# Perceiver block on one core: batch 0's last two head pairs ahead of batch 1's, and its distance stage inside the last step

## The chip, the cores and the metric

The kernel runs on one core of a Trainium2 chip. The metric is the device time of one execution in microseconds (us); less is better. The engines are TensorE (PE; its weight loads are listed as PEld), VectorE (DVE), ScalarE (ACT), GpSimd (POOL) and SyncE (SP), which issues all DMAs.

## The reference

Two batches of 256 tokens with 256 channels pass through three residual blocks. Cut to what matters:

```python
def reference(x, ctx, wq, wk, wv, wo, aq, ak, av, ao, Wg, bg, W1, b1, W2, b2):
    # 1 cross attention, 16 heads of 64, over 4096 context rows per batch
    q, k, v = heads(layernorm(x) @ wq), heads(ctx @ wk), heads(ctx @ wv)
    x = x + merge(softmax(q @ k.T / 8) @ v) @ wo
    # 2 self attention over 256 tokens, 16 heads of 16, by hyperbolic distance
    h = layernorm(x)
    q, k, v = heads(h @ aq.T), heads(h @ ak.T), heads(h @ av.T)
    denom = maximum((1 - |q|^2) * (1 - |k|^2), 1e-6)
    cosh_arg = maximum(1 + 2 * (|q|^2 + |k|^2 - 2 q @ k.T) / denom, 1)
    x = x + merge(softmax(-arccosh(cosh_arg)) @ v) @ ao.T
    # 3 eight experts; each token takes the one with the greatest gate
    h = layernorm(x)
    idx = argmax(softmax(h @ Wg + bg))
    y = gelu(h @ W1 + b1) @ W2 + b2        # per expert
    return x + take(y, idx)
```

## The kernel before

Every instruction is placed by hand: each engine has its own program, and semaphores link them.

**Cross attention** takes 16 steps, n = 0 to 15, one for a pair of heads `hp` and a batch `b`, in the order (0,0), (0,1), (1,0) up to (7,1). A step has 32 slots, one for 128 context rows. In a slot TensorE multiplies the scores (L1357, L1359), ScalarE takes their exponentials to fp32 (L1525) and in three slots of four to fp16 (L1523; in the fourth VectorE casts them, `split_p`, L1685), GpSimd subtracts the fp16 part from the fp32 one (L1826), and three slots later (LAG) TensorE multiplies probabilities and values, 12 short matmuls (`pv`, L1374 to L1379). Beside this TensorE projects the keys, the row maxima and the first values of the next step (`CHUNKS`, `MAX_AT`); scores have two PSUM banks and fp32 probabilities four buffers, so that no engine runs far ahead. The output of step n - 1 is normalised, turned, projected and added in slots 3 to 12 of step n.

The last step (n = 15, batch 1) prepares no further step. In its slots stand the layernorm of batch 0 (`LN_AT`), its transposes (`XT_AT`), the transposes of the four self attention weights (`TURN_AT`) and the split of the expert weights to fp16 high and low parts (`EXPERTS_AT`: high on ScalarE L768, low on VectorE L773, 8 each).

**Self attention** (`tail_pe`, `tail_act`, `tail_dve`, `tail_pool`) comes after the last `pv`. Per batch: *rows* i = 0 to 7, the projected queries and keys of four heads with their lengths (PE `qk` L570 and `lengths` L580, L584; ACT `squares` L788 and `rows` L797; DVE `low_rows` L965); *inverses*, twelve short VectorE instructions (L988 to L1004) for 1/(1 - length) in three bf16 parts; *placing* them (PE L605, ACT L808, DVE L1011), with a matrix `place` that GpSimd builds; 16 *distance units* m (PE L639, L641; DVE `ratios` L1028, L1031, two instructions of 128x512); then for each of four groups two roots (ACT L833, L835), their sum (POOL L457), logarithm and exponential (ACT L840, L848), and the `average` of the values with its transposes (L652, L662). `RATIO` names four buffers for eight groups. The rows of batch 1 are interleaved with the first units of batch 0. After that come output projection, a layernorm, the gate and the experts.

## Time and profile before

| | us |
|---|---|
| time, median of 3 runs | 1189.27 (1186.86 to 1191.82) |
| the profiled execution's own time | 1191.87 |
| its span, first to last instruction | 1190.1 |
| TensorE busy | 1082.1 (91% of the span) |
| ScalarE busy | 898.2 (75%) |
| VectorE busy | 814.0 (68%) |
| GpSimd busy | 696.8 (59%) |

Busy time is the union of an engine's instructions. The clock granted to TensorE is given as a share of full speed, 1.00 for 2.4 GHz and 0.50 for 1.2 GHz; its mean over the span is 0.947. Times of rows are counted from the start of the span.

### The profile page before, as it was taken

Reading aid. Unit: us, or ns where it says so; the run is one execution under the profiler, and the core shown is the slowest. Engines: PE = TensorE matmul, PEld = TensorE weight load, DVE = VectorE, ACT = ScalarE, POOL = GpSimd, SP = SyncE. Lnnn points to the kernel's source line nnn. Section 1 sums busy time; section 2 is a strip of 40 time slices with the busy share of each in tenths; the row PEclk is TensorE's granted clock in tenths of the full one; section 3 lists DMA queues with packets and bytes.
Section 4 is the critical chain, followed back from the end, with each engine's and each line's share of the span. In section 5 each row is a group of like instructions: output and inputs, shape, how many; then the busy total and the mean of one; then the engine's idle time right before and its main releaser. Section 6 shows DMA issues by size and latency. Waiting matters only on the chain.

```text
span 1190.1 us, 33353 instructions
## 1 busy us (share of the span) xinstructions
PE 1082.1 (91%) x13853; PEld 787.1 (66%) x13853; DVE 814.0 (68%) x1180; ACT 898.2 (75%) x1608; POOL 696.8 (59%) x603
## 2 busy tenths in 40 slices
PE   5789999999999999999999999999999878736698
PEld 3467777767677777676777777777777757412455
DVE  5878777686868686868686868777776445856322
ACT  5787888888888878788878787878887864478533
POOL 5567666666666666666666666666666780335023
...
DMA packets 32487, 42.00 MB, mean 35 GB/s; under 512 B 2874, under 2 KB 26962, under 8 KB 32338
## 3 DMA queue, kind: packets, MB, share of 16 engines
...
## 4 chain that ended last, share of the span: by engine, by line
PE 73%; DVE 10%; ACT 8%; issue 5%; POOL 3%; DMA 0%; DVEq 0%; ACTq 0%; POOLq 0%
PE ps L1261 12%; PE ps L1291 12%; PE ps L1357 8%; PE ps L1359 8%; PE ps L1374 6%; PE ps L1312 6%; PE ps L1379 5%; PE ps L1377 4%; DVE m_part L1659 3%; PE ps L704 2%; POOL psums L1826 2%; ACT probs L1525 2%; PE ps L722 2%; PE ps L1340 1%; PE ps L570 1%
## 5 line engine op out<-in xcount | busy, mean ns | idle before, releaser
L1826 POOL TENSOR_TENSOR psums<-probs 128x512 f16<-128x512 f32 x512 | 594.7, 1173 | 312.2 <-ACT probs L1525 171.2
L1525 ACT ACTIVATE probs<-ps 128x512 f32<-128x512 f32 x512 | 304.8, 599 | 52.7 <-PE ps L1359 52.0
L1659 DVE TENSOR_REDUCE m_part<-ps 128x2 f32<-128x1024 f32 x256 | 311.9, 1221 | 29.0 <-PE ps L1312 26.0
L1357 PE MATMUL ps<-q,k 128*128 128x256 f16 x1024 | 252.1, 273 | 5.6 <-ACT probs L1525 5.5
L1374 PE MATMUL ps<-v_sb,probs 128*128 128x65 f16 x2048 | 242.2, 194 | 15.4 <-issue 9.1
L1359 PE MATMUL ps<-q,k 128*128 128x256 f16 x1024 | 252.0, 273 | 0.0
L1523 ACT ACTIVATE probs<-ps 128x512 f16<-128x512 f32 x384 | 229.1, 597 | 22.2 <-PE ps L1359 18.3
L1377 PE MATMUL ps<-v_sb,probs 128*128 128x64 f16 x2048 | 240.1, 192 | 0.0
L1379 PE MATMUL ps<-v_sb,psums 128*128 128x65 f16 x2048 | 239.2, 194 | 0.0
L1374 PEld LDWEIGHTS ps<-v_sb,probs 128*128 128x128 f16 x2048 | 189.1, 98 | 68.8 <-issue 41.0
L1649 DVE TENSOR_TENSOR k<-ps,k 64x512 f16<-64x512 f32 x256 | 176.4, 689 | 51.8 <-ACT k L1480 47.6
L1480 ACT ACTIVATE k<-ps 64x512 f16<-64x512 f32 x256 | 151.4, 592 | 62.8 <-PE ps L1261 57.7
L1377 PEld LDWEIGHTS ps<-v_sb,probs 128*128 128x128 f16 x2048 | 191.0, 97 | 5.0
L1379 PEld LDWEIGHTS ps<-v_sb,psums 128*128 128x128 f16 x2048 | 191.1, 97 | 0.0
L1291 PE MATMUL ps<-wv_hi,ctx_lo 128*128 128x128 f16 x1024 | 184.9, 219 | 0.0
L1291 PE MATMUL ps<-wv_lo,ctx_hi 128*128 128x128 f16 x1024 | 184.7, 219 | 0.0
L1291 PE MATMUL ps<-wv_hi,ctx_hi 128*128 128x128 f16 x1024 | 184.5, 219 | 0.1
L1678 DVE TENSOR_TENSOR v_sb<-ps,v_sb 128x512 f16<-128x512 f32 x128 | 88.2, 690 | 107.2 <-ACT v_sb L1486 107.2
L1357 PEld LDWEIGHTS ps<-q,k 128*128 128x128 f16 x1024 | 100.2, 98 | 40.9 <-ACT probs L1525 6.5
L1359 PEld LDWEIGHTS ps<-q,k 128*128 128x128 f16 x1024 | 100.4, 98 | 34.3
L1312 PE MATMUL ps<-k,q 64*128 64x512 f16 x512 | 99.5, 386 | 12.0 <-DVE m_part L1659 12.0
L1291 PEld LDWEIGHTS ps<-wv_hi,ctx_hi 128*128 128x128 f16 x1024 | 100.4, 98 | 0.6 <-DVE v_sb L1678 0.3
...
## 6 DMA issues: line engine op xcount, KB each, us to landing
...
```

The costliest lines, as they stand in the source:

```text
L1291: mm = pe.matmul(ps[:, bank, t * P:(t + 1) * P], y[:, par, c, toks], w[:, par, c, :], start=(k == 0), stop=(k == 5))
L1312: mm = pe.matmul(ps[:, bank + 1 - h, :], q1[rows, par, h, t * P:(t + 1) * P], k1[rows, par, h, 512 * j:512 * (j + 1)], start=True, stop=True)
L1357: pe.matmul(ps[:, SC + s % 2, cols], k1[:, par, h, keys], q1[:, par, h, :], start=True, stop=False)
L1359: mm = pe.matmul(ps[:, SC + s % 2, cols], k2[:, par, h, keys], q2[:, par, h, :], start=False, stop=True)
L1374: pe.matmul(out, p_hi[:, s % NP, h, queries], value[:, XD:2 * XD + 1], start=(s == 0 and h == 0 and t == 0), stop=False, skip_group_check= ...
L1377: pe.matmul(ps[:, ACC, at:at + XD], p_hi[:, s % NP, h, queries], value[:, 0:XD], start=False, stop=False, skip_group_check=True)
L1379: mm = pe.matmul(out, p_lo[:, s % NP, h, queries], value[:, XD:2 * XD + 1], start=False, stop=(s == SLOTS - 1), skip_group_check=True)
L1523: nc.scalar.activation(p_hi[:, s % NP, :, :], scored, ACT.Exp, scale=XSCALE)
L1525: nc.scalar.activation(p_raw[:, s % NX, :, :], scored, ACT.Exp, scale=XSCALE) \
L1649: i = nc.vector.tensor_tensor(k1[other, par, h, keys], ps[rows, bank, :], k1[rows, par, h, keys], ALU.subtract)
L1659: nc.vector.tensor_reduce(m_part[:, j, t, :], ps[:, bank:bank + 2, :], AX.X, ALU.max) \
L1826: nc.gpsimd.tensor_tensor(p_lo[:, s % NP, :, :].rearrange("p h q -> p (h q)"), p_raw[:, s % NX, :, :].rearrange("p h q -> p (h q)"), p_hi[ ...
```

## The change

The order of the steps is the same up to step 11; then come (6,0), (7,0), (6,1), (7,1), so that batch 0 is complete one step earlier (`ORDER`, `DONE0` = 14). A step's buffers go by its parity now, not by its batch. GpSimd builds `place` (half as wide, 12 copies of 64 partitions) within step 13. Step 14, which is a full step with a successor, takes in addition batch 0's layernorm, the transposes of its rows and of the four weights, with the same PSUM bank (PM) for all. The weights' DMAs and the first expert matrix are issued ahead of step 15's key copies, the second one when four low parts are done. Step 15 takes batch 0's rows in slots 0 to 8, inverses (11 instructions now) in slots 9 to 11, placing in 14 and 15, and distance units 0 to 15 in slots 16 to 31. Four expert quarters are split in slots 1 to 7; the other high parts in slots 26 to 29, two low parts in 26 and 28, and the last two low parts after the step among batch 1's rows. What remains behind the last `pv` is batch 1's rows, inverses, placing and 16 units, and all roots, logarithms, exponentials and averages. Batch 0's roots stand among batch 1's rows on ScalarE; its averages stand among batch 1's units. `ratio` has eight buffers, and sums, logarithms and exponentials are made in place.

```diff
+ORDER = tuple((i // 2, i % 2) for i in range(STEPS - 4)) + tuple(
+    (hp, b) for b in range(B) for hp in (HP - 2, HP - 1))
+DONE0 = STEPS - 2
...
-TURN_AT = {20: 0, 23: 1, 27: 2, 29: 3}
-TURN_BANK = (MX, MX + 1, PK, MX)
-TURN_X = (PK, PM)
-RATIO = (0, 1, 3, 0, 1, 0, 2, 1)
-EXPERTS_AT = (13, 15, 18, 21, 27, 28, 30, 31)
+TURN_AT = {14: 0, 17: 1, 23: 2, 26: 3}
+XT_AT, VARIANCE_AT, ROOT_AT, NORMALISED_AT = 20, 13, 14, 15
+ZERO_AT = 5
+PLACE_AT = {4: None, 8: 0, 11: 1, 14: 2, 17: 3, 20: 4, 23: 5}
+INVERSES_AT = {9: (0, 1, 2, 3), 10: (4, 5, 6, 7), 11: (8, 9, 10)}
+PLACED_AT = {14: (0, 1), 15: (2, 3)}
+UNITS = 16
+UNIT_AT = {16 + m: m for m in range(UNITS)}
+HIGH_AT = {1: 0, 3: 1, 5: 2, 7: 3, 26: 4, 27: 5, 28: 6, 29: 7}
+LOW_AT = {1: 0, 3: 1, 5: 2, 7: 3, 26: 4, 28: 5}
+LATE_LOW_AT = {2: 6, 5: 7}
 OUT_BANKS = ((6, 7), (0, 1))
 XN_BANK, GATE_BANK = 2, 3
-AVERAGE_AT = (24, 27)
-PLACE_BANKS = ((0, 1), (4, 5))
-ROWS_AHEAD = 3
-LN_AT, ROOT_AT, XT_AT = 13, 15, 18
+ROOT_PART_AT = (1, 3, 5, 7)
+AVERAGE_AT = (24, 26, 28, 30)
+ROW_BANKS = ((4, 7), (4, 5, 7))
+PLACE_BANKS = (((4, 7), (3, 6)), ((4, 5), (4, 5)))
+PAIRS = ((3, 6), (0, 2))
 SPLIT_K_AT, SPLIT_V_AT = 16, 12
...
-        ratio = [m.rearrange("p (k h q) -> p k h q", k=2, h=4)
-                 for m in (k1_32[:, 6144:8192], lo32[:, 0:2048], v32[:, 0:2048],
-                           k2_32[:, 6144:8192])]
...
+        halves = [m[:, 4096:8192].rearrange("p (k s w) -> p s k w", k=2, s=2) for m in (k1_32, k2_32)]
+        ratio = [halves[0][:, 0, :, :], halves[1][:, 0, :, :],
+                 lo32[:, 4096:6144].rearrange("p (k w) -> p k w", k=2),
+                 lo32[:, 6144:8192].rearrange("p (k w) -> p k w", k=2),
+                 v32[:, 0:2048].rearrange("p (k w) -> p k w", k=2),
+                 halves[0][:, 1, :, :], halves[1][:, 1, :, :],
+                 hi32[:, 0:2048].rearrange("p (k w) -> p k w", k=2)]
...
-            sp.wait_ge(s_v, (STEPS - 1) * KCH)
-            for i, w in enumerate((aq, ak, av, ao)):
-                sp.dma_start(a_raw[:, i, :, :], w.rearrange("(t p) n -> p t n", p=P)).then_inc(s_aw, 16)
-            sp.wait_ge(s_sc, (STEPS - 1) * SLOTS)
-            for raw, w in ((w2_raw, w2), (w1_raw, w1)):
-                sp.dma_start(raw.rearrange("p (m n) -> p m n", n=F),
-                             w.rearrange("e (c p) n -> p (e c) n", p=P)).then_inc(s_ew, 16)
...
             if w == 0:
                 pe.wait_ge(s_aw, 4 * 16)
-                pe.wait_ge(s_red, STEPS * NU)
-                pe.wait_ge(s_ya, STEPS - 1)
+                pe.wait_ge(s_ya, DONE0)
+            else:
+                pe.wait_ge(s_ac, w)
             if w == 2:
...
+        def qk(pe, i, b):
+            w, g = divmod(i, 4)
+            if (b, i) == (0, 0):
+                pe.wait_ge(s_ac, 2)
+                pe.wait_ge(s_xc, NC + 1)
+                pe.wait_ge(s_vl, (STEPS - 1) * KCH + 2)
+                pe.wait_ge(s_red, STEPS * NU)
+            if (b, i) == (1, 0):
+                pe.wait_ge(s_xc, NC + 2)
+                pe.wait_ge(s_rt, 2 * 16)
+                pe.wait_ge(s_vl, STEPS * KCH)
+            if i >= len(ROW_BANKS[b]):
+                pe.wait_ge(s_lx, 8 * b + i - len(ROW_BANKS[b]) + 1)
+            for c in range(NC):
+                mm = pe.matmul(ps[:, row_bank(i, b), 0:TQ],
+                               aqk_T[:, w, c, 4 * g:4 * g + 4, :].rearrange("p h d -> p (h d)"),
+                               xnT[:, c, b * TQ:(b + 1) * TQ],
+                               start=(c == 0), stop=(c == NC - 1))
+            mm.then_inc(s_qk, 1)
+
...
+        def place_rows(pe, b, g):
+            if g == 0:
+                pe.wait_ge(s_iq, IQ * (b + 1))
+                pe.wait_ge(s_lx, 8 * (b + 1))
+            if (b, g) == (0, 0):
+                pe.wait_ge(s_tc, PLACED)
+                pe.wait_ge(s_ya, STEPS - 1)
+            for w in range(2):
+                if b == 0 and g >= 2:
+                    pe.wait_ge((s_pq, s_pk)[w], g - 1)
+                if b == 1 and g >= 1:
+                    pe.wait_ge((s_pq, s_pk)[w], 4 * b + g)
+                rows = slice(64 * w, 64 * w + 64)
+                for i in range(3):
+                    mm = pe.matmul(ps[:, PLACE_BANKS[b][g % 2][w], 0:TQ], place[rows, i, g, :],
+                                   inv_p[rows, i, :], start=(i == 0), stop=(i == 2))
+                mm.then_inc(s_pl, 1)
...
-            pe.wait_ge(s_tc, TC)
-            rows_step(0, 0)
             last_output()
-            for i in range(1, 9):
-                rows_step(i, 0)
-            pe.wait_ge(s_or, STEPS)
+            pe.wait_ge(s_ya, STEPS)
             transposes_batch(pe, 1)
-            values(1)
-            for i in range(ROWS_AHEAD):
-                rows_step(i, 1)
-            pe.wait_ge(s_tc, TC + 2)
-            place_rows(0)
...
+            for i in range(9):
+                multiply_rows(pe, i, 1)
+                if i == 0:
+                    pe.wait_ge(s_or, STEPS)
+                    values(1)
+            for g in range(4):
+                place_rows(pe, 1, g)
...
-            for m, gg, b, g, kt, jj in attn_units():
-                if m == 16:
-                    place_rows(1)
-                distances(m, b, g, kt, jj)
-                if ROWS_AHEAD + m < 9:
-                    rows_step(ROWS_AHEAD + m, 1)
+            for m, gg, b, g, kt, jj in attn_units()[16:]:
+                distances(pe, m, b, g, kt, jj)
                 if m in AVERAGE_AT:
-                    average(AVERAGE_AT.index(m), 0, AVERAGE_AT.index(m))
-            turn_average(0, 0, 0)
-            for g in range(2, 4):
-                average(g, 0, g)
-                turn_average(g - 1, 0, g - 1)
+                    i = AVERAGE_AT.index(m)
+                    average(i, 0, i)
+                    if i >= 1:
+                        turn_average(i - 1, 0, i - 1)
...
-            for b in range(B):
-                for g in range(4):
-                    if (b, g) == (0, 0):
-                        for i in range(ROWS_AHEAD, 9):
-                            rows_step(i, 1)
-                    roots(4 * b + g)
-                for g in range(4):
-                    logarithms(4 * b + g, g)
-                    if b == 0:
-                        take_placed(1, g)
-                    if (b, g) == (1, 2):
-                        take_turned_xn(1, 0, OUT_BANKS[0][0])
-                for g in range(4):
-                    weights(4 * b + g, g)
+            act.wait_ge(s_vone, 2)
+            take_turned_output()
+            take_values(0)
+            root_of_product(0)
+            root_of_variance(act, 2, slice(2, NT))
+            root_of_sum(0)
+            take_batch(act, 1)
+            take_rows(act, 0, 1)
+            take_values(1)
+            for i in range(1, 9):
+                take_rows(act, i, 1)
+                if i in ROOT_PART_AT:
+                    gg, part = divmod(2 + ROOT_PART_AT.index(i), 2)
+                    (root_of_product, root_of_sum)[part](gg)
+            roots(3)
+            for gg in range(3):
+                logarithms(gg)
+            for g in range(4):
+                take_placed(act, 1, g)
+            logarithms(3)
+            for gg in range(4):
+                weights(gg)
+            for gg in range(4, 8):
+                roots(gg)
+            for gg in range(4, 8):
+                logarithms(gg)
+                if gg == 6:
+                    take_turned_xn(1, 0, OUT_BANKS[0][0])
+            for gg in range(4, 8):
+                weights(gg)
...
+            def step(n):
+                par, (hp, b) = n % 2, ORDER[n]
+                if n + 2 < STEPS:
                     sp.wait_ge(s_q, n + 1)
                     sp.wait_ge(s_wkl, n + 1)
-                    load_wqk(b, hp + 1)
-                if prepares(hp, b):
+                    load_wqk(par, ORDER[n + 2][0])
+                if more_after(n):
                     at_least(sp, s_wvl, n)
-                    load_wv(1 - b, hp + b)
+                    load_wv(1 - par, ORDER[n + 1][0])
                 at_least(sp, s_yx, n - 1)
-                load_wo(b, hp)
-                if prepares(hp, b):
-                    copy_k2(n + 1, 1 - b)
-
-            for hp in range(HP):
-                step(hp, 0)
-                step(hp, 1)
+                load_wo(par, hp)
+                if n == DONE0:
+                    sp.wait_ge(s_v, DONE0 * KCH)
...
                         turn_weights(pe, TURN_AT[s])
+                    if not more:
+                        if s <= 8:
+                            multiply_rows(pe, s, 0)
+                        for i in PLACED_AT.get(s, ()):
+                            place_rows(pe, 0, i)
+                        if s in UNIT_AT:
+                            m, gg, _, i, kt, jj = units[UNIT_AT[s]]
...
-                    if s in EXPERTS_AT and not more:
-                        split_experts_high(act, EXPERTS_AT.index(s))
+                    if not more:
+                        if s <= 8:
+                            take_rows(act, s, 0)
+                        if s in HIGH_AT:
+                            split_experts_high(act, HIGH_AT[s])
+                        for i in PLACED_AT.get(s, ()):
+                            take_placed(act, 0, i)
...
+                    if n == DONE0 and s == VARIANCE_AT:
+                        dve.wait_ge(s_ya, DONE0)
+                        variance(1, slice(0, 2))
+                    if n == DONE0 and s == NORMALISED_AT:
+                        normalised(1, slice(0, 2))
+                    if not more:
+                        if 1 <= s <= 8:
+                            low_rows(dve, s - 1, 0)
+                        for k in INVERSES_AT.get(s, ()):
+                            inverses(dve, 0, k)
+                        if s in LOW_AT:
+                            split_experts_low(dve, LOW_AT[s])
+                        for i in PLACED_AT.get(s, ()):
+                            take_placed_keys(dve, 0, i)
+                        if s in UNIT_AT:
+                            m, gg, _, i, kt, jj = units[UNIT_AT[s]]
+                            ratios(dve, m, gg, 0, kt, jj)
...
```

`multiply_rows`, `take_rows`, `low_rows`, `inverses`, `take_placed` and `distances` are the functions of before, moved out of the tail and called from both places.

On VectorE, the first slots of step 15 before the change (n = 15, probabilities, output and values alone):

```order
L1685 CAST probs<-probs 128x512 [waits s_pv,s_exp]
L1693 COPY o_acc<-ps 128x264 [waits s_on,s_pv]
L1698 RECIPROCAL o_rcp<-o_acc 128x4 [waits s_or]
L1701 TENSOR_TENSOR o_norm<-o_acc,o_rcp 128x2x2x64 [waits s_tt,s_rs]
L1685 CAST probs<-probs 128x512 [waits s_pv,s_exp]
L1678 TENSOR_TENSOR v_sb<-ps,v_sb 128x8x64 [waits s_vc]
L1685 CAST probs<-probs 128x512 [waits s_pv,s_exp]
L1678 TENSOR_TENSOR v_sb<-ps,v_sb 128x8x64 [waits s_vc]
L1711 TENSOR_TENSOR x_sb<-x_sb,ps 128x512 [waits s_ya,s_yx]
```

and with it:

```order
L1703 CAST probs<-probs 128x512 [waits s_pv,s_exp]
L953 SCALAR_TENSOR_TENSOR k<-ps,vecs,k 128x256 [waits s_qx]
L773 SCALAR_TENSOR_TENSOR k<-ctx_hi,k 128x1024 [waits s_eh]
L953 SCALAR_TENSOR_TENSOR k<-ps,vecs,k 128x256 [waits s_qx]
L1711 COPY o_acc<-ps 128x264 [waits s_on,s_pv]
L953 SCALAR_TENSOR_TENSOR k<-ps,vecs,k 128x256 [waits s_qx]
L773 SCALAR_TENSOR_TENSOR k<-ctx_hi,k 128x1024 [waits s_eh]
L1716 RECIPROCAL o_rcp<-o_acc 128x4 [waits s_or]
L1719 TENSOR_TENSOR o_norm<-o_acc,o_rcp 128x2x2x64 [waits s_tt,s_rs]
L953 SCALAR_TENSOR_TENSOR k<-ps,vecs,k 128x256 [waits s_qx]
L1703 CAST probs<-probs 128x512 [waits s_pv,s_exp]
L1696 TENSOR_TENSOR v_sb<-ps,v_sb 128x8x64 [waits s_vc]
```

The low rows (L953) and the low parts of the experts (L773) now stand between the casts, the output of step 14 and the values. Later in the same step, from slot 18 on before the change:

```order
L1685 CAST probs<-probs 128x512 [waits s_pv,s_exp]
L773 SCALAR_TENSOR_TENSOR ctx_hi<-k,ctx_hi 128x1024 [waits s_eh]
L1678 TENSOR_TENSOR v_sb<-ps,v_sb 128x8x64 [waits s_vc]
L1685 CAST probs<-probs 128x512 [waits s_pv,s_exp]
L773 SCALAR_TENSOR_TENSOR ctx_hi<-k,ctx_hi 128x1024 [waits s_eh]
L1685 CAST probs<-probs 128x512 [waits s_pv,s_exp]
L1678 TENSOR_TENSOR v_sb<-ps,v_sb 128x8x64 [waits s_vc]
L773 SCALAR_TENSOR_TENSOR ctx_hi<-k,ctx_hi 128x1024 [waits s_eh] x2
L1685 CAST probs<-probs 128x512 [waits s_pv,s_exp]
L773 SCALAR_TENSOR_TENSOR ctx_hi<-k,ctx_hi 128x1024 [waits s_eh] x2
L1693 COPY o_acc<-ps 128x264 [waits s_on,s_pv]
```

and the end of placing with units 0 to 4 (slots 15 to 20) with it:

```order
L986 CAST wqk_raw<-ps 128x256 [waits s_pl] x2
L1003 TENSOR_SCALAR k<-ps 128x512 [waits s_sc,s_dd]
L1005 SCALAR_TENSOR_TENSOR k<-ps,k 128x512 [waits s_rt]
L1703 CAST probs<-probs 128x512 [waits s_pv,s_exp]
L1003 TENSOR_SCALAR k<-ps 128x512 [waits s_dd]
L1005 SCALAR_TENSOR_TENSOR k<-ps,k 128x512 [waits s_rt]
L1003 TENSOR_SCALAR k<-ps 128x512 [waits s_dd]
L1005 SCALAR_TENSOR_TENSOR k<-ps,k 128x512 [waits s_rt]
L1696 TENSOR_TENSOR v_sb<-ps,v_sb 128x8x64 [waits s_vc]
L1003 TENSOR_SCALAR k<-ps 128x512 [waits s_dd]
L1005 SCALAR_TENSOR_TENSOR k<-ps,k 128x512 [waits s_rt]
L1003 TENSOR_SCALAR k<-ps 128x512 [waits s_sc,s_dd]
```

Each slot from 16 on now has two instructions of a unit that wait for TensorE (s_dd), and later casts and values are queued behind them. On ScalarE, from the last exponentials on, before the change:

```order
L1525 ACTIVATE probs<-ps 128x512 [waits s_lo]
L768 ACTIVATE ctx_hi<-k 128x1024
L780 ACTIVATE psums<-ps 128x16x16 [waits s_vp,s_vone]
L780 ACTIVATE psums<-ps 128x16x16
L1493 ACTIVATE o_turn<-ps 128x256 [waits s_yx,s_tt]
L788 ACTIVATE ctx_lo<-ps 128x256 [waits s_qk] x2
L797 ACTIVATE k<-ps,vecs 128x256 [waits s_nm]
L788 ACTIVATE ctx_lo<-ps 128x256 [waits s_sl,s_qk]
L797 ACTIVATE k<-ps,vecs 128x256 [waits s_nm]
```

and with it:

```order
L1507 ACTIVATE o_turn<-ps 128x256 [waits s_yx,s_tt,s_vone]
L809 ACTIVATE psums<-ps 128x16x16 [waits s_vp]
L809 ACTIVATE psums<-ps 128x16x16
L820 ACT_TABLE_LOAD [waits s_pv]
L820 ACTIVATE probs<-k 128x2048 [waits s_rt]
L751 ACTIVATE rstd<-var 128x2 [waits s_ln]
L823 ACTIVATE k<-k,vecs 128x2x1024
L507 ACTIVATE xnT<-ps 128x2x256 [waits s_xt]
L780 ACTIVATE ctx_lo<-ps 128x256 [waits s_sl,s_qk]
L809 ACTIVATE psums<-ps 128x16x16 [waits s_vp]
L809 ACTIVATE psums<-ps 128x16x16
L780 ACTIVATE ctx_lo<-ps 128x256 [waits s_sl,s_qk]
```

The output of step 15 is taken first, then the first root of batch 0 (L820) with its table load stands ahead of the layernorm's root (L751), and the rows of batch 1 follow.

## Rows read from the trace of the kernel before

**Rows 1.** Stretches: length, busy us of PE, PEld, DVE, ACT, POOL, clock, DMA.

```profile
863.70:920.70 57.00, 56.06 (x800) 41.80 (x799) 41.85 (x57) 46.20 (x89) 36.88 (x33) 1.00 0.18 45
920.70:974.50 53.80, 41.47 (x678) 36.27 (x676) 26.91 (x38) 43.89 (x78) 42.91 (x37) 0.91 0.24 77
1029.80:1091.00 61.20, 29.39 (x254) 12.59 (x258) 46.12 (x67) 43.20 (x28) 27.38 (x6) 0.50 0.00 0
1091.00:1190.10 99.10, 79.51 (x471) 47.59 (x463) 27.04 (x72) 49.26 (x59) 27.46 (x18) 0.81 0.02 6
```

**Rows 2.** Groups in step 15: busy, mean ns, idle before.

```profile
L773 DVE SCALAR_TENSOR_TENSOR ctx_hi<-k,ctx_hi 128x1024 f16<-128x1024 f32 x8 | 12.1, 1512 | 8.5 <-ACT ctx_hi L768 8.5
...
L752 ACT ACT_TABLE_LOAD x1 | 1.3, 1283 | 0.0
```

**Rows 3.** TensorE in step 15 in order of time: start, duration, idle before.

```profile
930.23 0.20 PE L1374 MATMUL ps<-v_sb,probs 128*128 128x65 f16 x1 [1.10 <-POOL psums L1826]
...
930.60 0.27 PE L1357 MATMUL ps<-q,k 128*128 128x256 f16 x1
...
930.93 0.27 PE L1359 MATMUL ps<-q,k 128*128 128x256 f16 x1
...
946.17 0.39 PE L1357 MATMUL ps<-q,k 128*128 128x256 f16 x1 [4.03 <-ACT probs L1525]
```

**Rows 4.** TensorE in the rows of batch 0, then of batch 1.

```profile
987.77 1.03 PE L570 MATMUL ps<-xnT,ctx_lo 128*128 128x256 f32 x4
...
989.50 1.03 PE L570 MATMUL ps<-xnT,ctx_lo 128*128 128x256 f32 x4
...
998.33 0.60 PE L505 MATMUL ps<-ident,xn 128*128 128x128 f32 x4
...
1011.08 2.07 PE L570 MATMUL ps<-xnT,ctx_lo 128*128 128x256 f32 x4
...
1014.79 0.83 PE L639 MATMUL ps<-k 32*128 32x256 f16 x6
```

**Rows 5.** VectorE: inverses of batch 0, placing, one inverse of batch 1.

```profile
999.01 0.41 DVE L988 TENSOR_SCALAR ctx_lo<-ps 128x256 f32<-128x256 f32 x1
...
1004.45 0.42 DVE L1004 TENSOR_TENSOR ctx_lo<-ctx_lo 128x256 f32<-128x256 f32 x1
...
1008.48 0.42 DVE L1011 CAST k<-ps 128x256 bf16<-128x256 f32 x1 [0.59 <-PE ps L605]
...
1032.43 3.29 DVE L992 TENSOR_TENSOR ctx_lo<-ctx_lo 128x256 f32<-128x256 f32 x1
```

**Rows 6.** VectorE in batch 1's units, and an average among them.

```profile
1072.14 0.68 DVE L1028 TENSOR_SCALAR k<-ps 128x512 f32<-128x512 f32 x1
...
1073.46 0.68 DVE L1028 TENSOR_SCALAR k<-ps 128x512 f32<-128x512 f32 x1
...
1079.22 0.42 DVE L1038 COPY ctx_lo<-ps 128x256 f32<-128x256 f32 x1 [0.39 <-PE ps L652]
1080.19 0.69 DVE L1028 TENSOR_SCALAR v_sb<-ps 128x512 f32<-128x512 f32 x1 [0.54 <-PE ps L641]
```

**Rows 7.** ScalarE and GpSimd in the units of batch 0 and the exponentials.

```profile
1030.81 4.64 POOL L457 TENSOR_TENSOR k<-probs,k 128x2048 f32<-128x2048 f32 x1 [50.16 <-ACT k L835]
...
1042.03 1.91 ACT L833 ACTIVATE probs<-k 128x2048 f32<-128x2048 f32 x1 [7.33 <-DVE k L1031]
...
1067.00 7.31 ACT L848 ACTIVATE k<-k 128x2048 f32<-128x2048 f32 x4
```

**Rows 8.** From the last pv to batch 1's layernorm.

```profile
980.67 0.66 ACT L780 ACTIVATE psums<-ps 128x256 f32<-128x256 f32 x2 [9.79 <-POOL psums L449]
...
983.48 0.69 DVE L1711 TENSOR_TENSOR x_sb<-x_sb,ps 128x512 f32<-128x512 f32 x1 [7.83 <-PE ps L1340]
...
990.17 0.74 DVE L1591 BATCH_NORM_STATS2 stats<-x_sb 128x6 f32<-128x256 f32 x2
...
992.73 0.74 DVE L1610 TENSOR_SCALAR xn<-x_sb,mv,rstd 128x256 f32<-128x256 f32 x2
```

608 lines of the change are left out of this document (285 added, 323 removed).

## The prediction

> **What bounds the kernel now.** I read the stretches first, then TensorE's timeline in the last step, then all engines in order of time behind the last pv. In step 14 TensorE is busy 56.1 of 57.0 us at clock 1.00 [rows 1]: a full step is bound by TensorE, and whatever it is given there is added to the time. Step 15 (920.7 to 974.5) is not: TensorE is busy 41.5 of 53.8 us, and none of the four others is full [rows 1]. One wait of 4.03 us stands in it, where the layernorm and its two table loads of 1.28 us hold up the exponentials [rows 2, 3]. Behind the last pv (974.5) the engines take turns. From 1029.8 to 1091.0 TensorE is busy 29.4 of 61.2 us at clock 0.50, VectorE 46.1, ScalarE 43.2, GpSimd 27.4 [rows 1]: VectorE works on units while ScalarE waits 7.33 us for four of them [rows 7], then ScalarE works while VectorE waits. So the end is set by a serial chain of VectorE and ScalarE that lasts 116.5 us from the last pv to the last unit, and 99.1 us more to the end of the span [rows 1]. Those 99.1 us (roots of the last group, logarithms, exponentials, output, gate, experts) hold the same operations before and after the change; I leave them as they are. So I need three terms: step 14, step 15, and the stretch from the last pv to the last unit.
>
> **Steps 0 to 13: nothing.** The order of batches changes which context columns are read, not how many. In step 13 GpSimd gets a memset and 12 small copies; it is busy only 36.9 of 57 us in a full step [rows 1], so they lie beside TensorE. If that cover were gone they would cost at most the 4.9 us between the last pv and GpSimd's memsets (974.5 to about 979.4; ScalarE's 9.79 us wait in [rows 8] contains them).
>
> **Step 14: +3 us.** TensorE gets 20 transposes. Four of them took 0.60 us with their drain [rows 4], some 0.44 in a row: 5 x 0.44 = 2.2 us, all on the path, as TensorE is the bound. ScalarE gets two table loads (2.6), five evictions of 0.5 to 0.6 (2.8) and the root: 46.2 + 5.7 = 52 of 59 us, so it has room on average, but in slot 14 it waits for the transposes and then reloads its table. TensorE has two slots of 1.8 us before it needs that exponential, which covers most of it; I take 0.8 us. Bounds: 2.2 (all covered) and 6 (the 4.03 us wait of [rows 3] comes back in part). The transposes of the rows stand five slots behind the layernorm now and wait for nothing. SP issues four weight loads and a 2 MB load ahead of step 15's key copies; the copies' data exist only from the middle of step 14, so they are not delayed.
>
> **Step 15: +17 us.** Slots 0 to 8. TensorE's work in a slot: pv 0.35 (930.23 to 930.60 with its issue) and scores 0.44 (four at 0.11) [rows 3], and one cycle of rows, 1.73 (987.77 to 989.50) [rows 4]: 2.5 us, and 0.64 more in two slots with values. Now the links. `qk` of cycle i + 1 needs the bank that low row i - 1 frees (two banks, three in the tail), and that row goes from TensorE's length over ScalarE (0.47) to VectorE (0.48). ScalarE also has exponentials (0.95) and in four slots an expert quarter (about 1.0); in slot 3 VectorE takes the old output behind a low part, and pv waits for it about 1 us. By laying these out slot by slot I get 24 us for the nine slots. Slots 9 to 15: the inverses are a VectorE chain, 999.01 to 1005.2 before [rows 5], 5.9 us with one instruction less, plus a cast and values; they must be done at slot 14, for placing. Two groups of placing in a slot take about 1 us (one lasted 1.01 [rows 5]); 15 us for seven slots. Slots 16 to 31: a unit costs VectorE 1.32 us (1072.14 to 1073.46) [rows 6]. 16 x 1.33 = 21, four casts 1.8, two values 1.4, two low parts at 1.5 each 3.0 [rows 2], and 1.5 us because unit 8 writes where context values are still read until slot 25: 29 us. TensorE's share of such a slot (0.8 and 0.5 for a unit) fits. Three more pv: 3. Sum 24 + 15 + 29 + 3 = 71, against 53.8: +17. Bounds: TensorE's own sum, about 56 us with all that it is given, plus waits of 8 (+10), and +26 if each slot of the rows takes 3.2 us and each unit's slot 2.0. The stall of 4.03 us is gone from this step and is already in the difference.
>
> **From the last pv to the last unit: 116.5 becomes 77 us, -39.5.** (a) Batch 1's xnT is ready 12 us behind the last pv: before, the output was added at 984.2 (9.7 us) after a wait for GpSimd's place work [rows 8]; without that work I take 7.5, then 3.3 for the layernorm (990.17 to 993.47) [rows 8], 0.6 for transposes, 0.6 for the eviction. (b) Rows of batch 1 alone: nine cycles of 1.73 are 15.6, values 2; ScalarE's four root parts of 1.9 [rows 7] fit into two cycles each with little over, and TensorE has just idled, so some of it runs at clock 0.50; I add 2.4: 20 us. (c) Then ScalarE has two roots, a table load and three logarithms before it takes a placed row: 3.9 + 1.3 + 5.7 = 11 us; VectorE's inverses (5.9, and two waits of 2.9, see below) run beside that and are level with it. (d) Placing 4 x 1.05 and the first unit: 5 us. (e) 16 units, 21.2 us; four averages among them: one cost VectorE 1.4 us (from 1078.8, the end of a unit, to the start of the next at 1080.19) [rows 6], with a transpose behind it at clock 0.50 2.0: 1.4 + 3 x 2.0 = 7.4. Sum 12 + 20 + 11 + 5 + 28.6 = 76.6. What is saved is batch 0's rows, inverses, placing and 16 units, whose roots now run where ScalarE idled. Bounds: 69 (root parts hidden, averages 1.4 each) and 91 (the two rivals on this stretch together).
>
> One rule speaks against (c). The inverse at 1032.43 took 3.29 us instead of the 0.42 of its like [rows 5], and it lies within a GpSimd addition of 4.64 us that began at 1030.81 [rows 7]: 2.9 us of waiting. My sum has two such waits. The Trainium skill, page "SBUF — State Buffer", section "🔬 SBUF: two separate sides", states an exclusive lock: a VectorE operation with two SBUF inputs and a GpSimd operation that reads SBUF block one another for the whole instruction. By that rule, the trace agrees, all five such instructions that now stand in this stretch (two late low parts, three inverses) can wait, not two; that is the port rival below.
>
> **The sum.** +3 + 17 - 39.5 = -19.5. On the profiled execution (span 1190.1, own time 1191.87) that is a span of 1170.6 and a time of 1172.4; its own time lies 2.6 us over the median of 1189.27, so against the median I say 1170.
>
> **Rivals.** *Slower: TensorE falls to 1.2 GHz in step 15.* Its place is slots 0 to 8, where it now waits for ScalarE and VectorE in each slot. At clock 0.50 a cycle of rows took 3.71 us (1011.08 to 1014.79) [rows 4] against 1.73: 8 x 2.0 = 16, and scores and pv double, 9 x 0.8 = 7: +23, 1193 us. It decides from 19 us on, that is if some four fifths of these slots run so. For it: in the old units, clock 0.50 stayed for 61 us. Against it: in step 15 TensorE is busy 77% of the time and the mean clock is still 0.91 [rows 1]; it fell once, with the 4.03 us idle stretch [rows 3], and the new step keeps it busier. Chance 0.10, of which half is partial and ends within 0.5%.
>
> *The rows in the tail run at 1.2 GHz.* They begin after some 4 us of idle TensorE, and ScalarE's root parts keep interrupting. 8 x (3.71 - 1.95) = 14: 1184 us. Against it: they are almost back to back on TensorE. Chance 0.10.
>
> *The port rival.* Three more waits of 2.9 us: +9, 1179 us. Against it: GpSimd is free for much of (b). Chance 0.08.
>
> *More than I say.* Links in step 15 overlap better than my slot by slot layout (+12), and (b) to (e) take 70: 1158 us. Chance 0.13.
>
> *The forecast itself,* 1163 to 1178: 0.59.
>
> **Numbers.** 0.5% is 5.9 us, about what a measurement of this kernel can tell from no change: below 1183.3 is faster, above 1195.2 slower. Of the slower rival 0.05 counts as slower, 0.05 as same; of the 1.2 GHz rows 0.04 as same. Faster 0.86, same 0.09, slower 0.05. The range 1160 to 1184 leaves out half of the better case (0.07) and the slower rival (0.10).
>
> **What the profile will show.** Step 14 lasts 60 us instead of 57, with ScalarE's wait in slot 14. Step 15 lasts about 71, at clock near 1.00, with 2.7 us a slot at first and 1.8 in the units. From the last pv to the last unit 77 us, ScalarE without a 7 us wait among batch 0's roots, and 99 us after it. I am wrong if TensorE shows clock 0.50 in step 15, if casts queued behind units starve GpSimd and pv, or if the 99 us stretch, which I did not cost, moves.

## The result and the profile after

The changed kernel takes 1170.82 us (median of four runs, 1167.91 to 1171.87) against 1189.43 (1186.86 to 1191.82, four runs) on the same chip: a ratio of 0.984, 95% interval 0.9812 to 0.9868. That is 18.6 us less; 19.4 were forecast, from 1189.27 to 1170. The profiled execution took 1171.87 us, its span is 1170.2, and 1170.6 was forecast for the span.

The windows of the changed kernel, with the columns of [rows 1]: step 14, step 15, then three pieces of step 15, then pieces of the tail, and last the stretch behind the last unit.

```profile
864.00:928.10 64.10, 60.01 (x818) 45.12 (x817) 46.09 (x69) 51.00 (x97) 38.12 (x37) 0.97 0.12 33
928.10:1000.20 72.10, 65.55 (x875) 54.10 (x874) 50.00 (x79) 48.21 (x90) 38.34 (x33) 0.93 0.10 31
...
928.10:952.90 24.80, 24.20 (x256) 21.05 (x255) 12.80 (x20) 19.99 (x40) 11.08 (x10) 1.00 0.01 2
952.90:967.60 14.70, 11.77 (x170) 9.88 (x167) 10.72 (x20) 8.40 (x18) 7.98 (x7) 0.88 0.46 145
967.60:1000.20 32.60, 29.59 (x453) 23.17 (x454) 26.48 (x41) 19.82 (x34) 19.29 (x16) 0.90 0.01 2
1000.20:1013.90 13.70, 7.83 (x28) 5.83 (x28) 4.45 (x16) 7.10 (x9) 5.71 (x9) 0.75 0.01 2
1013.90:1030.90 17.00, 13.74 (x64) 11.62 (x62) 7.29 (x13) 15.54 (x23) 6.61 (x2) 0.99 0.00 0
1030.90:1046.30 15.40, 4.17 (x32) 1.97 (x36) 10.96 (x13) 10.91 (x11) 6.96 (x2) 0.50 0.00 0
1046.30:1070.80 24.50, 18.80 (x200) 8.47 (x192) 22.24 (x37) 22.29 (x13) 9.58 (x3) 0.70 0.01 2
1070.80:1170.20 99.40, 75.11 (x437) 46.52 (x437) 26.09 (x70) 49.25 (x59) 26.91 (x18) 0.81 0.02 6
```

Against [rows 1]: step 14 is 7.1 us longer, step 15 18.3 us longer, the 116.5 us from the last pv to the last unit are 70.6, and what follows them lasts 99.4 instead of 99.1. TensorE is busy 65.6 of 72.1 us in step 15, where it was busy 41.5 of 53.8: the work went to where four engines had had room. All terms: +0.2 ahead of step 14, +7.1, +18.3, -45.9, +0.3, together -20.0, which is the difference of the spans (1190.1 and 1170.2) to rounding.

In step 14 three waits of TensorE stand that were not there before. TensorE in step 14 of the changed kernel:

```profile
894.13 0.39 PE L1313 MATMUL ps<-k,q 64*128 64x512 f16 x2 [0.77 <-DVE m_part L1677]
...
895.92 0.28 PE L1362 MATMUL ps<-q,k 128*128 128x256 f16 x1 [0.28 <-ACT probs L1539]
...
900.84 0.61 PE L1313 MATMUL ps<-k,q 64*128 64x512 f16 x2 [2.42 <-DVE m_part L1677]
```

The largest waits for VectorE's maxima (L1677), since they free the PSUM pair of the scores. So ScalarE and VectorE are read next, each in order of time:

```profile
891.49 1.28 ACT L751 ACT_TABLE_LOAD   x1
892.78 0.20 ACT L751 ACTIVATE rstd<-var 128x2 f32<-128x2 f32 x1
...
893.49 1.28 ACT L1537 ACT_TABLE_LOAD   x1
...
895.75 0.60 ACT L1500 ACTIVATE v_sb<-ps 128x512 f16<-128x512 f32 x1
```

```profile
892.76 1.23 DVE L1677 TENSOR_REDUCE m_part<-ps 128x2 f32<-128x1024 f32 x1
896.39 0.69 DVE L1696 TENSOR_TENSOR v_sb<-ps,v_sb 128x512 f16<-128x512 f32 x1 [2.40 <-ACT v_sb L1500]
897.00 0.15 DVE L1622 RECIPROCAL rstd<-rstd 128x2 f32<-128x2 f32 x1
...
897.58 1.02 DVE L1625 TENSOR_SCALAR newton<-newton 128x2 f32<-128x2 f32 x1
...
898.83 0.73 DVE L1628 TENSOR_SCALAR xn<-x_sb,mv,rstd 128x256 f32<-128x256 f32 x2
899.48 1.22 DVE L1677 TENSOR_REDUCE m_part<-ps 128x2 f32<-128x1024 f32 x1
```

This is one chain over three engines. The two table loads, 2.6 us, make ScalarE late with the values; VectorE stands idle for them (2.40 us), then does the root's Newton step and the normalisation (897.00 to 899.5) and only then takes the maxima on which TensorE waits 2.42 us. Behind that wait the granted clock is 0.50 from 900.8 to 904.2. One instruction of the Newton step, L1625, takes 1.02 us for two numbers per partition, where its neighbours take 0.16. It starts within a subtraction of GpSimd and ends 0.02 us after it:

```profile
897.42 1.16 POOL L1863 TENSOR_TENSOR psums<-probs 128x512 f16<-128x512 f32 x1 [0.31 <-ACT probs L1539]
```

### The profile page after: what moved, and what is told of

Same layout as the page of the kernel before. It is cut to its first block, busy times and chain, and to the rows that moved or that the text cites. A ratio compares the mean times of both kernels' runs of the same rounds, so it can differ in the third digit from the quotient of the medians.

```text
span 1170.2 us, 33359 instructions
## 1 busy us (share of the span) xinstructions
PE 1072.6 (92%) x13853; PEld 786.2 (67%) x13853; DVE 810.0 (69%) x1178; ACT 898.6 (77%) x1608; POOL 692.8 (59%) x603
## 4 chain that ended last, share of the span: by engine, by line
PE 73%; DVE 11%; ACT 8%; issue 5%; POOL 2%; DMA 0%; DVEq 0%; ACTq 0%; POOLq 0%
PE ps L1262 12%; PE ps L1292 12%; PE ps L1362 8%; PE ps L1364 8%; PE ps L1379 6%; PE ps L1313 6%; PE ps L1384 5%; PE ps L1382 4%; DVE m_part L1677 3%; PE ps L703 2%; PE ps L721 2%; ACT probs L1539 2%; POOL psums L1863 2%; PE ps L1345 1%; PE ps L1236 1%
## 5 line engine op out<-in xcount | busy, mean ns | idle before, releaser
L1539 ACT ACTIVATE probs<-ps 128x512 f32<-128x512 f32 x512 | 304.1, 598 | 53.8 <-PE ps L1364 53.1
L1677 DVE TENSOR_REDUCE m_part<-ps 128x2 f32<-128x1024 f32 x256 | 312.0, 1221 | 28.7 <-PE ps L1313 25.7
L1494 ACT ACTIVATE k<-ps 64x512 f16<-64x512 f32 x256 | 151.4, 592 | 62.5 <-PE ps L1262 56.8
```

Source lines behind the costliest of these rows:

```text
L1539: nc.scalar.activation(p_raw[:, s % NX, :, :], scored, ACT.Exp, scale=XSCALE) \
L1677: nc.vector.tensor_reduce(m_part[:, j, t, :], ps[:, bank:bank + 2, :], AX.X, ALU.max) \
```

## The experiments

**The same kernel again (e8_again)**, no edit, five rounds.

> The changed kernel itself once more, on the same chip as the next three. All theories: 1168 to 1172 us. Step 14 takes 64.1 us where a stretch of clock 0.50 follows the 2.43 us wait on the maxima, and 62.6 where none does.

1166.09 us (1162.05 to 1167.23), ratio 0.9793, 0.9763 to 0.9824: below the 1168 to 1172 that were expected. The profiled execution shows clock 1.00 throughout steps 14 and 15:

```profile
864.00:926.00 62.00, 57.92 (x815) 43.67 (x814) 46.40 (x68) 50.53 (x96) 37.61 (x36) 1.00 0.10 27
926.00:995.20 69.20, 61.31 (x874) 51.20 (x873) 49.67 (x79) 47.86 (x89) 38.15 (x33) 1.00 0.10 32
```

From first exponential to first exponential step 14 lasts 62.6 us here and 64.1 in the first profile, step 15 69.3 and 72.0, and the rest of the span is equal to 0.1 us (170.0). So two executions of one program differ by some 4 us in these two steps, with the stretches at clock 0.50 in the one and none in the other. Single executions are compared with that in mind: a difference of 4 us in the time of one execution is no finding, one of 1 us in a stretch at the same clock is. The stretch ahead of step 14, which no edit below touches, also differs: step 14 starts between 862.6 us (e5_filler) and 866.7 us (e11_four).

**The normalisation one slot later (e1_norm16).** Is it VectorE's order or ScalarE's tables that hold TensorE up?

```diff
-XT_AT, VARIANCE_AT, ROOT_AT, NORMALISED_AT = 20, 13, 14, 15
+XT_AT, VARIANCE_AT, ROOT_AT, NORMALISED_AT = 20, 13, 14, 16
```

> One constant: the second half of batch 0's layernorm on VectorE stands in slot 16 of step 14, behind the maxima, instead of slot 15 ahead of them. Theory 1 (VectorE's queue: maxima late behind normalised, which stood behind values that waited for ScalarE): the 2.43 us wait of TensorE on the maxima disappears, step 14 goes from 64.15 to about 61.7 us, 1168.5 us in all. Rival (the surplus of step 14 is TensorE's transposes or ScalarE's table loads alone): step 14 stays at 64.1, 1171.

1167.32 us (1166.53 to 1168.69), ratio 0.9803, 0.979 to 0.9816. Step 14 lasts 61.5 us at clock 1.00, 1.1 less than in e8_again. The 2.42 us wait did not vanish but moved two slots on and fell to 1.32. TensorE and VectorE of this kernel:

```profile
903.62 0.39 PE L1313 MATMUL ps<-k,q 64*128 64x512 f16 x2 [1.32 <-DVE m_part L1677]
```

```profile
899.72 0.74 DVE L1628 TENSOR_SCALAR xn<-x_sb,mv,rstd 128x256 f32<-128x256 f32 x2
...
902.24 1.23 DVE L1677 TENSOR_REDUCE m_part<-ps 128x2 f32<-128x1024 f32 x1
```

So the move is worth 1.1 us, but not all of it is the place in the queue. The instruction of the Newton step that took 1.02 us beside GpSimd's subtraction now runs while GpSimd is idle:

```profile
899.31 0.17 DVE L1625 TENSOR_SCALAR newton<-newton 128x2 f32<-128x2 f32 x1
```

That is 0.85 us less work on VectorE ahead of the maxima, and no kernel here separates it from the order. What is left of the wait I put down to VectorE's added work, some 4 us (891.20 to 892.7 and 897.0 to 899.5 in the changed kernel), and its 2.4 us of idle time, all within five slots; that is an argument, no run shows it alone.

**Without the table loads (e2_copy_root).** The root of batch 0's variance becomes a copy, which needs no other table; batch 0's layernorm is not the reference's here. One profiled execution, as for every kernel below with a single time.

```diff
-            nc.scalar.activation(rstd[:, tiles], var[:, tiles], ACT.Sqrt).then_inc(s_sd, 1)
+            nc.scalar.activation(rstd[:, tiles], var[:, tiles], ACT.Copy if i == 1 else ACT.Sqrt).then_inc(s_sd, 1)
```

> The square root of batch 0's variance in step 14 is replaced by a copy (its layernorm is then not the reference's), so ScalarE loads no table there: two loads of 1.28 us less. Theory 1 (late values come from the two loads, and the maxima behind them): step 14 falls to about 61.5 us. Rival (only the place of normalised on VectorE counts): step 14 stays within 0.5 us of 64.15. If the transposes alone make the surplus: no change either.

1164.05 us; step 14 lasts 61.15 us, 1.4 less than in e8_again at the same clock. The wait on the maxima is 1.43 us with no table load at all:

```profile
901.18 0.39 PE L1313 MATMUL ps<-k,q 64*128 64x512 f16 x2 [1.43 <-DVE m_part L1677]
```

So the loads alone don't make the wait: they are worth 1.0 to 1.4 us of step 14, and moving VectorE's part is worth 1.1 (e1), L1625's wait for GpSimd included. Here L1625 still takes 1.02 us. The remainder over the 57.0 of before, 4.1 us, is the 2.2 of transposes and about as much in waits (0.76 and 1.43).

**The 16 units back behind step 15 (e3_units_tail), and everything back (e4_all_tail).** These take the core of the change apart. Of e3 the core is

```diff
-UNIT_AT = {16 + m: m for m in range(UNITS)}
+UNIT_AT = {}
...
             transposes_batch(pe, 1)
+            for m, gg, b, g, kt, jj in attn_units()[:16]:
+                distances(pe, m, b, g, kt, jj)
```

with the ratios on VectorE at the same place and the first root behind batch 1's layernorm. e4 also moves rows, inverses and placing of batch 0:

```diff
             last_output()
+            for i in range(9):
+                multiply_rows(pe, i, 0)
+            for g in range(4):
+                place_rows(pe, 0, g)
```

> Batch 0's 16 distance units go back behind the last pv (after batch 1's transposes), rows, inverses and placing of batch 0 stay in step 15. Theory 1 (a unit costs little in step 15, and VectorE's whole 1.32 us behind it): step 15 falls from 72.0 to 64 us, the stretch behind it grows by 22 us: 1184 us. Rival (units beside the scores cost as much as alone): 1171, within 3 us.

> Rows, inverses, placing and units of batch 0 all go back behind the last pv, one after the other; order of steps and step 14 stay. Theory 1 (the gain is the overlap of this work with step 15, net of 18 us): step 15 takes 47 to 49 us, the stretch behind it grows by 48: about 1194 us, slower than the kernel before, whose rows and units of the two batches were interleaved. Rival (the gain comes from the order of the pairs and ScalarE's roots in batch 1's rows): 1175 to 1180.

e3 takes 1182.91 us (1181.18 to 1186.47), ratio 0.9933, 0.9915 to 0.9951; e4 1196.47 (1195.35 to 1196.93), ratio 1.0042, 1.0028 to 1.0055. The windows of e4, step 15 and then last pv to last unit:

```profile
927.80:974.80 47.00, 37.90 (x661) 32.63 (x658) 24.14 (x24) 38.95 (x70) 42.41 (x33) 0.98 0.15 47
974.80:1097.50 122.70, 81.25 (x531) 49.95 (x530) 76.53 (x133) 64.32 (x73) 28.82 (x15) 0.70 0.00 1
```

What each part costs in step 15 and behind it, from the lengths of these stretches in the three kernels:

| part of batch 0 | cost in step 15 | cost behind it | gain |
|---|---|---|---|
| rows, inverses, placing (e4 to e3) | 46.7 to 62.5: 15.8 | 122.7 to 93.3: 29.4 | 13.6 |
| 16 units (e3 to after) | 62.5 to 72.0: 9.5 | 93.3 to 70.6: 22.7 | 13.1 |

The 16 units cost VectorE about 21 us wherever they stand [rows 6], and TensorE about 0.6 us each at clock 1.00 (1062.13 to 1062.75); in step 15 they lengthen the step by 9.5 us, behind it by 22.7. Some of the 9.5 is clock: with the 69.3 us of e8_again, at clock 1.00, it would be 6.8, so the gain of the units is 13 to 16 us. The whole gain comes from this overlap, some 27 us, about half of it from either part. The lengths are as expected for both kernels (step 15 64 and 47 to 49, the stretch behind it 22 and 48 longer), except that e4's stretch behind it is 52 longer. Laid out one after the other as in e4, the same work is about 5 us slower than the kernel before: step 14 is 7.1 us longer (the layernorm), step 15 7.0 shorter, and the tail 6.2 longer; behind the last unit it is 1.8 shorter (97.3).

**TensorE kept busy in the 4.66 us gap (e5_filler).** Behind the output TensorE waits for batch 1's layernorm, and its next matmuls run at 1.2 GHz. 18 matmuls that nothing reads fill the gap.

```diff
             last_output()
+            pe.wait_ge(s_rt, 2 * 16)
+            for _ in range(18):
+                pe.matmul(ps[:, PM, :], wv_hi[:, 1, 0, :],
+                          q1[:, 0, :, :].rearrange("p h q -> p (h q)"), start=True, stop=True)
```

> 18 idle matmuls of 128x512 into a free bank stand behind the last output projection, in TensorE's wait of 4.66 us for batch 1's layernorm. If the clock of 0.50 in the stretch behind that wait costs time (theory of the 1.2 GHz rival, in small): transposes, first rows and values of batch 1 take 2 us less, and the last unit ends 2 us earlier. Rival (the links through ScalarE and VectorE set this stretch, or the matmuls themselves come in the way): no change or up to 1 us later.

TensorE in the changed kernel, and then in e5_filler:

```profile
1008.50 1.09 PE L501 MATMUL ps<-ident,xn 128*128 128x128 f32 x4 [4.66 <-DVE xn L1628]
...
1010.27 2.07 PE L525 MATMUL ps<-xnT,ctx_lo 128*128 128x256 f32 x4 [0.69 <-ACT xnT L507]
```

```profile
1002.07 4.05 PE L640 MATMUL ps<-q,wv_hi 128*128 128x512 f16 x18
...
1006.88 0.63 PE L501 MATMUL ps<-ident,xn 128*128 128x128 f32 x4 [0.77 <-DVE xn L1632]
...
1008.20 1.13 PE L525 MATMUL ps<-xnT,ctx_lo 128*128 128x256 f32 x4 [0.69 <-ACT xnT L507]
```

The granted clock stays 1.00, the transposes fall from 1.09 to 0.63, the first cycle's xnT matmuls from 2.07 to 1.13; the rows end 2.0 us and the last unit 1.8 us earlier, as expected. The time, 1164.23, is lower by more than that, because the stretch behind the last unit is 95.1 us instead of 99.4 and step 14 starts 1.4 us earlier. Its second half, the experts, lasts 54.6 us in this execution and 58.5 in the changed kernel's.

**Is that second gain from the clock too (e9_filler2)?** Ten such matmuls behind the first logits, ahead of the experts, and nothing in the first gap.

```diff
             logits(0)
+            for _ in range(10):
+                pe.matmul(ps[:, 4, :], wv_hi[:, 1, 0, :],
+                          q1[:, 0, :, :].rearrange("p h q -> p (h q)"), start=True, stop=True)
             turn_normalised(1)
```

> 10 idle matmuls of 128x512 stand behind the first logits, in TensorE's wait for batch 1's last layernorm, ahead of the experts. Clock theory (of the 58.5 us from the first hidden matmul to the end, 4 are lost at clock 0.50 in the first ten us): this stretch takes 54.6 us and the time falls by 3 to 4 us against the changed kernel on this chip. Rival (the first hidden matmuls wait for other engines, or the clock falls all the same): no change.

1168.84 us (1166.88 to 1171.76), ratio 0.9824, 0.9794 to 0.9854: no gain over e8_again. TensorE around the start of the experts:

```profile
1101.87 2.33 PE L693 MATMUL ps<-q,wv_hi 128*128 128x512 f16 x10
...
1104.88 0.63 PE L592 MATMUL ps<-ident,xn 128*128 128x128 f32 x4 [0.68 <-DVE k L1023]
...
1108.40 4.45 PE L706 MATMUL ps<-k 128*128 128x512 f16 x12
```

The clock is 1.00 from the filler to 1109.0. There, 0.6 us into the experts, it falls to 0.50 for 3.4 us, so the first twelve matmuls still take 4.45 us (4.82 in the changed kernel), and the experts' stretch is 58.1 us. That is the second half of the rival: the clock falls all the same. What the filler did bring stands ahead of the experts: from the transposes L592 to the first expert matmul 3.5 us instead of 5.2. In the profiled execution that is covered by steps 14 and 15, 1.5 and 2.1 us longer than in e8_again.

Is the 54.6 in e5_filler clock at all? The windows answer it. In the changed kernel and then in e5_filler:

```profile
1119.30:1126.00 6.70, 6.70 (x21) 3.56 (x20) 1.36 (x3) 1.83 (x3) 1.53 (x2) 0.50 0.00 0
```

```profile
1110.60:1126.00 15.40, 14.11 (x86) 8.45 (x84) 3.35 (x5) 6.70 (x12) 4.62 (x4) 1.00 0.00 1
```

In the changed kernel the clock is 0.50 for the first 4.1 us of the experts, rises, and falls a second time for 6.7 us (in e9_filler2 for 6.5). In e5_filler it is 0.50 for the first 2.7 us and 1.00 from then on. That is 8.1 us less at half the clock; TensorE is busy in all of them, so by estimate they are worth about 4.0 us, and the stretch is 3.9 shorter. Of the thirteen profiled kernels three show no second fall, and they are the three at 54.5 to 54.8 us (e2, e5, e7); the ten others, the kernel before among them, show one of 3 to 7 us and take 57.4 to 58.6. So the difference is the clock, though not at the start of the experts, where e9_filler2 set out to hold it. TensorE's waits for other engines are the same with and without the second fall (1.29 us for ScalarE and 1.2 for GpSimd); why it comes in the one and not in the other, and whether an edit has part in it, no run here shows.

**The low halves of the experts out of the units (e6_lows_late).**

```diff
-LOW_AT = {1: 0, 3: 1, 5: 2, 7: 3, 26: 4, 28: 5}
-LATE_LOW_AT = {2: 6, 5: 7}
+LOW_AT = {1: 0, 3: 1, 5: 2, 7: 3}
+LATE_LOW_AT = {0: 4, 2: 5, 4: 6, 6: 7}
```

> The two low expert parts that stand in slots 26 and 28 of step 15 go behind the step, among batch 1's rows (four there instead of two). Theory 1 (VectorE is the bound of the unit slots, TensorE waits 2.5 us for it at units 12 to 14): step 15 takes 2.5 us less, and the parts are hidden in VectorE's waits of the rows: 2 us less in all. Rival (they delay low rows, or GpSimd holds the port): step 15 2.5 us less, the stretch behind it as much or more longer.

Step 15 lasts 68.3 us (69.3 in e8_again, 72.0 in the first profile) and the tail is 1.05 longer. But 69.3 was measured at clock 1.00 throughout, while e6's step 15 has a stretch at 0.50 among the last units. Two pairs of kernels with the same stretch at 0.50, 33 to 37 us into the step, say more: 70.8 us in e1 and e2, with the parts in the units, and 68.3 and 68.5 in e10 and e11, without them. So the move is worth 2.4 us in step 15, as theory 1 has it, and costs 1.05 behind it, because the parts are not hidden among the rows: 1.4 us net. The single time, 1169.03 us, can't show that.

**Placing ahead of the roots and logarithms (e7_placed_first).** Term (c) says that ScalarE's queue holds up placing, and the port rival that GpSimd holds up VectorE. This kernel changes both.

```diff
-            roots(3)
-            for gg in range(3):
-                logarithms(gg)
             for g in range(4):
                 take_placed(act, 1, g)
-            logarithms(3)
+            roots(3)
+            for gg in range(4):
+                logarithms(gg)
```

> ScalarE takes batch 1's placed rows ahead of the roots of group 3 and the logarithms, so that GpSimd has no addition for group 3 while VectorE makes the inverses. Port theory: the two scalar operations of 1.25 and 4.49 us fall to at most 1.5 us together with what is left of group 2's addition, and batch 1's first unit starts 3.5 to 4.5 us earlier. Rival (the length of these operations is not GpSimd's doing): they stay as long and the unit starts when it did. For the whole time: ScalarE is the next bound and has the same work left, so I expect no more than 1 us of gain, and 1 us of loss as likely.

VectorE and GpSimd at the inverses in the changed kernel, and then in e7_placed_first, where one GpSimd addition stands instead of two:

```profile
1032.24 1.25 DVE L968 TENSOR_SCALAR last_raw<-last_raw,rvec 128x256 f32<-128x256 f32 x1
1033.53 4.49 DVE L970 TENSOR_SCALAR last_raw<-last_raw,rvec 128x256 f32<-128x256 f32 x1
1038.05 0.48 DVE L972 SCALAR_TENSOR_TENSOR last_raw<-last_raw,rvec 128x256 f32<-128x256 f32 x1
```

```profile
1028.82 9.04 POOL L459 TENSOR_TENSOR ctx_lo<-probs,ctx_lo 128x2048 f32<-128x2048 f32 x2 [2.38 <-ACT ctx_lo L823]
```

```profile
1029.93 1.23 DVE L967 TENSOR_SCALAR last_raw<-last_raw,rvec 128x256 f32<-128x256 f32 x1
1031.20 0.35 DVE L969 TENSOR_SCALAR last_raw<-last_raw,rvec 128x256 f32<-128x256 f32 x1
```

```profile
1026.51 4.50 POOL L459 TENSOR_TENSOR ctx_lo<-probs,ctx_lo 128x2048 f32<-128x2048 f32 x1 [2.35 <-ACT ctx_lo L823]
```

The two additions of the changed kernel end at about 1033.3 and 1037.9, and the two TENSOR_SCALARs behind the reciprocal end 0.15 us after each; in e7 the addition ends at 1031.0, the first TENSOR_SCALAR at 1031.2, and the second takes the bare 0.35. So VectorE waits for GpSimd, for 5.0 us in the changed kernel (0.9 and 4.1) and 0.9 in e7. Placing is done and the first unit starts 2.8 us earlier in e7 (3.5 to 4.5 expected). But batch 0's exponentials come later, VectorE waits 4.13 us at the first average, and the last unit ends 1.1 us later than in the changed kernel. From there to the first expert it takes 46.8 us instead of 40.9, because ScalarE then still has its last root and four logarithms, and the exponentials stand behind them:

```profile
1074.38 1.91 ACT L820 ACTIVATE probs<-ctx_hi 128x2048 f32<-128x2048 f32 x1 [0.67 <-POOL k L459]
```

So the edit costs 7 us, where no more than 1 us of loss was expected. The time, 1171.64, hides it: in this execution the experts take 54.8 us instead of 58.5, and steps 14 and 15 have less of clock 0.50. The gain on VectorE's chain is lost on ScalarE's, which is the longer one from here on.

**The edits of e1, e5 and e6 together (e10_three), and those with e9's (e11_four).** They repeat the edits above word for word.

> Three edits on the changed kernel: normalised in slot 16, four low expert parts behind step 15, 18 idle matmuls in TensorE's wait for batch 1's layernorm. If the gains add up: 1.1 (step 14, at equal clock) + 1.3 (low parts, net) + 1.8 (clock in the rows) and sometimes the 1.5 us of clock in step 14: 4 to 5 us less than the changed kernel, about 1166. Rival (ScalarE has no slack behind the rows): the 1.3 is lost, 1167.5.

> The three edits and the 10 idle matmuls ahead of the experts: another 3 to 4 us if the clock theory holds, about 1162 to 1163; as the kernel with three edits if not.

e10_three takes 1161.54 us (1157.68 to 1162.36), ratio 0.9754, 0.9724 to 0.9784; e11_four 1163.18 (1157.83 to 1165.75), ratio 0.9764, 0.9731 to 0.9797. The windows of e10_three, steps 14 and 15, the tail to the last unit, and the rest:

```profile
864.00:925.50 61.50, 58.51 (x818) 44.05 (x817) 45.91 (x69) 50.89 (x97) 37.82 (x37) 1.00 0.11 31
925.50:993.80 68.30, 62.65 (x875) 52.10 (x874) 47.27 (x78) 47.92 (x90) 37.39 (x33) 0.98 0.11 33
993.80:1062.90 69.10, 46.84 (x332) 28.31 (x331) 49.77 (x80) 55.84 (x54) 29.40 (x15) 0.78 0.00 1
1062.90:1160.10 97.20, 71.75 (x437) 44.84 (x437) 26.04 (x70) 49.23 (x59) 26.85 (x18) 0.84 0.02 6
```

That is the fastest version found, 4.5 us under e8_again, which ran on the same chip; 4 to 5 us were expected. The profiled executions differ by 5.1: 1.1 in step 14, 1.05 in step 15 (with a stretch at clock 0.50 that e8_again lacks), 1.5 in the tail and 2.15 behind the last unit, where none of the three edits stands, against 0.7 ahead of step 14. So part of it is the clock of those executions. The fourth edit shows no gain (3 to 4 us were expected, if the clock theory held); the 2.5 us by which e11's profiled span is longer lie ahead of step 14, where the two kernels are the same.

## Why the prediction was right, and where its terms were off

**The whole.** -19.5 was forecast for the span and -20.0 came. Two terms were off in opposite directions by about as much, +4.1 and -6.4, so part of the agreement is luck. The same kernel on another chip measured 23.5 us under the kernel before (e8_again, 1166.09 against 1189.59), 4 more than forecast.

**Step 14, +3: too small.** It was +7.1, or +5.6 at clock 1.00 (62.6 us). The 2.2 us of transposes stood. The step that failed is "0.8 us" for ScalarE's wait: TensorE waited 0.77 + 0.28 + 2.42 = 3.5 us, and the largest was for VectorE. I had counted the layernorm's matmuls and its ScalarE work and had costed VectorE's part at nothing, without naming a cover, in the one step that TensorE bounds. e2 shows what the table loads are worth, 1.0 to 1.4 us; e1 shows 1.1 for VectorE's part, of which up to 0.85 is VectorE's own wait for GpSimd at L1625. The other 1.5 us are clock, 0.50 behind the long wait, which the sum did not hold for this step. The upper bound of 6 was too low in the first profile.

**Step 15, +17: right.** +18.3, or +15.5 in e8_again. Slots 0 to 8 took 24.8 (forecast 24), 9 to 15 14.7 (15), the rest 32.6 (29 + 3). The sum of the slots held. In the first piece TensorE is busy 24.2 of 24.8 us, so that piece is TensorE's own work, and the links through the other engines cost almost nothing there.

**From the last pv to the last unit, -39.5: it was -45.9.** (a) 10.1, forecast 12. (b) 18.9 (20). (c) 12.2 (11): VectorE was the bound there and ScalarE waited 1.73 us for it, where I had them level. (d) 5.7 (5). (e) 23.7 (28.6), which is the step that was mis-sized. I had given three of the averages 2.0 us each, with the transpose behind them at clock 0.50. VectorE around the first average and around a later one:

```profile
1059.47 0.42 DVE L1039 COPY ctx_lo<-ps 128x256 f32<-128x256 f32 x1 [0.39 <-PE ps L655]
1060.43 0.69 DVE L1003 TENSOR_SCALAR k<-ps 128x512 f32<-128x512 f32 x1 [0.54 <-PE ps L583]
...
1063.09 0.41 DVE L1039 COPY ctx_lo<-ps 128x256 f32<-128x256 f32 x1
1063.42 0.68 DVE L1003 TENSOR_SCALAR k<-ps 128x512 f32<-128x512 f32 x1
```

The first costs the 1.4 us of [rows 6]; the later ones cost 0.33, the start of the copy to the start of the next unit. Their sums were ready, as the average's matmuls ran while VectorE worked, and from 1061.2 the clock was 1.00. Before, the weights were late and the clock low when the one in [rows 6] was read: a row read in a starved stretch was carried into one that was not.

**The 99.1 us that were left alone:** 99.4. That held for this pair of executions. In the other kernels it is 93.8 to 101.7, of which up to 4 us are the second fall of the clock in the experts, and 6 in e7 the order on ScalarE.

**The rivals.** *TensorE at 1.2 GHz in step 15:* not in slots 0 to 8, where the rival had it (clock 1.00). But the sign that I gave did show: clock 0.50 in two stretches further on (962.3 to 965.7, 993.0 to 999.8), mean 0.93, which cost 2.7 us against e8_again. *The rows at 1.2 GHz:* only the first transposes and the first cycle, 2 us, as e5 shows; from 1013.5 to 1030.5 the clock is 1.00. *The port rival:* the blocking is real, but its extra is about 5 us and not 3 x 2.9 more, about the 5.8 that the sum held. It struck other instructions than I named. I had taken "two SBUF inputs" for the condition, and of the five such instructions only one touched an addition (a low part that started 0.17 us before its end and took 1.26 us instead of 1.22); the blocked TENSOR_SCALARs have one tensor input, in SBUF. VectorE's low rows, which read one input from PSUM and one from SBUF, took their usual 0.48 us within the additions (1022.51, 1029.14). The Trainium skill, page "SBUF — State Buffer", section "Who interferes with whom", has the other half: a tensor-scalar can run in a two-port mode, which takes the same lock. The trace agrees, 4.49 us beside an addition and 0.35 without, and so does L1625 in step 14, 1.02 beside a subtraction and 0.17 without (e1). *More than I say:* its tail (70) came true, if the 70 is read as the whole stretch, for (b) to (e) alone were forecast at 64.6; its step 15 did not.

**What stays open.** Why the clock falls a second time within the experts in ten of the thirteen profiled kernels and not in three, and why the stretches at clock 0.50 in steps 14 and 15 come in one execution of a program and not in another. Neither was taken further. Also not shown: how the 1.1 us of e1 divide between the order and the wait for GpSimd.
